# Cross attention: an output product with a new head sums the older head first and asks for the newer head's low part only at its last product

## The reference

```python
x = _rmsnorm(hidden_states, ln_weight)
h_q = (x @ w_q.T).reshape(b, lq, H, DH)                # H = 32, DH = 128, lq = lk = 128, b = 8
h_k = (key_value_states @ w_k.T).reshape(b, lk, H, DH)
h_v = (key_value_states @ w_v.T).reshape(b, lk, H, DH)
score = jnp.einsum('bqhd,bkhd->bhqk', h_q, h_k) + position_bias[None]
score = jax.nn.softmax(jnp.where(m, score, -jnp.inf), axis=-1)
attn = jnp.einsum('bhqk,bkhd->bqhd', score, h_v).reshape(b, lq, H * DH)
out = attn @ w_out.T
return hidden_states + out
```

## Time and profile before

| | |
|---|---|
| median of 3 runs | 1169.56 us (1166.43 to 1171.3) |
| profiled execution | 1164.94 us, of which span 1163.1 us |
| PE busy, PEld busy | 1113.6 us, 986.4 us |
| DVE, ACT, POOL busy | 536.7, 545.2, 223.6 us |
| mean granted PE clock | 0.987 of full |

### The profile page before, as it was taken

One profiled execution on the slowest core, in us unless ns is written; L12 is line 12 of the kernel. 1 busy time (PEld: TensorE's weight loads), 2 busy tenths in 40 slices (PEclk: granted clock), 3 DMA queues, 4 the chain that ended last, 5 costly groups with the idle time before them and its releaser, 6 DMA issues.

```text
span 1163.1 us, 20141 instructions
## 1 busy us (share of the span) xinstructions
PE 1113.6 (96%) x6904; PEld 986.4 (85%) x6904; DVE 536.7 (46%) x2002; ACT 545.2 (47%) x1342; POOL 223.6 (19%) x231
## 2 busy tenths in 40 slices
PE   4899999899999999999999999999999999999897
PEld 4899998798888888888888888888888888888785
DVE  3467777545344343434342434343343434343584
ACT  4687877434444444434443434434443434344412
POOL 5444544231010101010110101010101010111052
PEclk9899998899999999999999999999999999999999
DMA  3400100032020110101020202020211101000001
GB/s 138 158 10 11 47 2 2 28 137 78 1 77 25 52 58 18 59 18 59 18 72 5 77 0 77 0 77 1 75 35 41 59 18 59 18 23 1 1 2 72
DMA packets 16600, 49.63 MB, mean 43 GB/s; under 512 B 2480, under 2 KB 4912, under 8 KB 16048
## 3 DMA queue, kind: packets, MB, share of 16 engines
q1 hardware_dynamic: 16272, 44.93, 11.4%
q0 software_dynamic: 288, 4.19, 0.9%
HBM read 47.02 MB, written 2.10 MB: 42 GB/s over the span
## 4 chain that ended last, share of the span: by engine, by line
PE 88%; DVE 4%; ACT 3%; issue 3%; POOL 1%; DMA 1%; SPq 0%; ACTq 0%; POOLq 0%; DVEq 0%
PE bank L595 63%; PE bank L1238 5%; PE bank L1221 5%; PE bank L490 4%; PE bank L533 3%; PE bank L1260 3%; PE bank L1228 2%; PE bank L521 1%; DVE at_lo L1011 1%; ACT at_hi L861 1%; DMA stage<-in_wq 1%; PE bank L1298 1%; DVE sm L419 1%; POOL rot L290 0%; ACT pr L345 0%
## 5 line engine op out<-in xcount | busy, mean ns | idle before, releaser
L745 POOL TENSOR_TENSOR bm<-mask,bias 128x512 f32<-128x512 f32 x64 | 97.7, 1527 | 747.1 <-DVE nmx L999 483.9
L847 ACT ACTIVATE pr<-sm,nmx 128x128 f32<-128x128 f32 x256 | 99.8, 391 | 180.4 <-DVE nmx L999 180.2
L1011 DVE TENSOR_TENSOR at_lo<-bank,at_hi 128x512 fp32r<-128x512 f32 x64 | 44.2, 691 | 257.0 <-ACT at_hi L861 257.0
L1017 DVE TENSOR_TENSOR acc<-acc,bank 128x512 f32<-128x512 f32 x128 | 87.8, 687 | 138.9 <-PE bank L595 138.9
L840 ACT COPY v<-bank 128x256 f32<-128x256 f32 x128 | 47.8, 373 | 128.3 <-PE bank L595 77.0
L595 PE MATMUL bank<-wv_hi,cT_hi 128*128 128x256 f32 x512 | 92.5, 303 | 2.9 <-DVE wv_lo L985 2.9
L595 PE MATMUL bank<-wo_hi,at_hi 128*128 128x512 f32 x256 | 82.6, 404 | 11.1 <-DVE at_lo L1011 5.9
L595 PE MATMUL bank<-wv_lo,cT_hi 128*128 128x256 f32 x512 | 82.3, 283 | 0.0
L595 PE MATMUL bank<-wv_hi,cT_lo 128*128 128x256 f32 x512 | 82.2, 283 | 0.0
L834 ACT COPY kT<-bank 128x512 f32<-128x512 f32 x64 | 37.6, 588 | 90.7 <-PE bank L595 90.7
L419 DVE CUSTOM_DVE_ANT_0 sm<-bank,causal 128x128 f32<-128x128 f32 x256 | 58.8, 285 | 45.3 <-issue 41.8
(11 more groups left out here) (181 smaller groups left out, 2298.2 us busy)
## 6 DMA issues: line engine op xcount, KB each, us to landing
qk_raw<-in_wqk SPq DMA_DIRECT2D x32, 512.0 KB, 4.6
v_raw<-in_wv SPq DMA_DIRECT2D x16, 512.0 KB, 4.4
o_raw<-in_wo SPq DMA_DIRECT2D x16, 512.0 KB, 3.4
xT_raw<-in_xT SPq DMA_DIRECT2D x8, 256.0 KB, 2.8
acc<-in_x POOLq DMA_DIRECT2D x1, 2048.0 KB, 8.2
stage<-in_cT POOLq DMA_DIRECT2D x1, 2048.0 KB, 12.8
bias<-in_bias SPq DMA_DIRECT2D x16, 128.0 KB, 3.1
out<-acc SPq DMA_DIRECT2D x8, 256.0 KB, 2.0
```

What stands on the lines that cost most here:

```text
L745: nc.gpsimd.tensor_tensor(bm[:, s % 2], mask[:, HALF * (s // HG):HALF * (s // HG + 1), :], bias[:, s % HG:s % HG + 1, :].broadcast_to([P, ...
L847: e = nc.scalar.activation(pr[:, s % 2, k], sm[:, s % 2, k], ACT.Exp, bias=nmx[:, s % 2, k:k + 1], accum_out=sums[:, s % 2, k:k + 1])
L1011: nc.vector.tensor_tensor(at[1][:, s // HG, s % HG], PO[:], f32(at[0][:, s // HG, s % HG]), ALU.subtract).then_inc(s_al, 1)
L1017: nc.vector.tensor_tensor(acc[:, b], acc[:, b], PX[b % 2][:], ALU.add).then_inc(s_acc, 1)
```

## The change

`output` no longer calls `product`. It issues the same six matmuls, head by head: the three parts of head i = 0, then the three parts of head i = 1. Where it is the first output with a new head (`fresh`), the wait for `s_al` ahead of all six is gone; in its place the fourth matmul waits for `s_ah` and the sixth, which is the only one that reads the new head's low part, for `s_al`. All 128 outputs get the new order, 32 of them the new waits.

```diff
-            def output(b, half):
+            def output(b, half, fresh=None):
+
                 tok = slice((b - half * HALF) * T, (b - half * HALF + 1) * T)
-                product(nc, PX[b % 2][:], [[(at[p][:, half, i, tok], wo[q][:, i, :]) for i in range(HG)]
-                                           for p, q in PARTS]).then_inc(s_out, 1)
+                for i in range(HG):
+                    for p, q in PARTS:
+                        if fresh is not None and i == HG - 1 and (p, q) == PARTS[0]:
+                            pe.wait_ge(s_ah, fresh)
+                        if fresh is not None and i == HG - 1 and p == 1:
+                            pe.wait_ge(s_al, fresh)
+                        ins = nc.tensor.matmul(PX[b % 2][:], at[p][:, half, i, tok], wo[q][:, i, :],
+                                               start=i == 0 and (p, q) == PARTS[0],
+                                               stop=i == HG - 1 and (p, q) == PARTS[-1])
+                ins.then_inc(s_out, 1)
...
                     def out(j):
-                        if j == 0 and s in (0, 2):
-                            pe.wait_ge(s_al, n)
                         if j == 0 and s == 2:
                             pe.wait_ge(s_wo, g + 1)
-                        output((HALF + 2 * s + j) % B, 0 if s >= 2 else 1)
+                        output((HALF + 2 * s + j) % B, 0 if s >= 2 else 1, n if j == 0 and s in (0, 2) else None)
...
                     transpose_x2(0)
                     transpose_x2(1)
-                    pe.wait_ge(s_al, n)
                     for j in range(HALF):
                         pe.wait_ge(s_acc, 2 * n - 5 + j)
-                        output(HALF + j, 1)
+                        output(HALF + j, 1, n if j == 0 else None)
```

## The result

| | before | changed |
|---|---|---|
| median | 1169.58 us (4 runs, 1166.43 to 1171.3) | 1152.07 us (4 runs, 1148.18 to 1152.59) |
| ratio to before | | 0.9846, 95% interval 0.9816 to 0.9876 |
| profiled execution | 1164.94 us, span 1163.1 | 1152.29 us, span 1150.5 |
| first to last scores of the attention | 854.51 us | 835.61 us |

The change makes the kernel 17.5 us faster by the medians, 1.5%. The forecast was 1150.5 us and 19.0 us less.

What follows compares the result with a forecast made beforehand. PE, busy 96% of the span, was taken as the bound, so only its pauses could shrink. 15 x 0.66 + 15 x 0.61 + 0.26 = 19.3 us, or 18.6 by places, taken as 19.0, gave 1150.5 us; range 1145 to 1157.

Steps and rivals of the forecast that it cites:

- The price of a wait: Pause before the output product: 0.66 us in steps s = 0, 0.61 us in s = 2, against the s = 1 step.
- Who is late: Output products wait for DVE's at_lo, both in the 15 named waits and in the 15 unnamed ones of s = 2.
- The wait for the high part: At the output's fourth matmul, due at 519.80; high part complete at 518.79, 1.0 us before, so no cost.
- the satisfied waits in mid-stream: Waits already met inside the output's matmul stream: taken as free, at most 0.08 us for each of the two.
- the new order: Operands alternating between high and low parts over 768 matmuls: no cost, 3.8 us on either side.
- The cover of the low part: At the output's sixth matmul: low part released 0.37 us before the weight load is due, so the wait costs nothing.
- The sum: Total saved on PE's waits before outputs: 19.3 us by step lengths, 18.6 us by places, taken as 19.0 us.
- The end, counted at nothing: The 32nd wait, at the attention's end: nothing saved, since PE waits 0.73 us for xnT_lo a few us later.
- Weight loads uncovered by satisfied waits: Rival: each of 31 outputs gives back 2 x 0.08 us, 5.0 us in all, 1155.5 us; chance 0.08.
- A repeated load dropped: Rival: the second load of each head's high part falls away, 4.4 us more gained, 1146 us; chance 0.04.
- Half of the waits something else: Rival: unnamed waits of s = 2 are not for at_lo, so only 9.9 us go, 1159.7 us; chance 0.04.
- A slower order: Rival: part changes between neighbouring matmuls cost 0.08 us each, 61 us over 768, 1212 us; chance 0.04.

Runs made afterwards that it cites:

- order_only: Changed kernel keeping the new matmul order, but with the wait for the low part back ahead of all six; 1168.52 us, ratio 1.0003 to before.
- before_late_one: Kernel before the change, with one added DVE operation ahead of each low part; 1186.71 us, ratio 1.0127 to before.
- waits_only: Changed kernel with the old matmul order, waiting for the high part at the second matmul and the low part at the sixth; 1151.89 us, ratio 0.9864.
- low_at_fourth: Changed kernel with the low part awaited at the fourth matmul instead of the sixth, no wait for the high part; 1151.43 us, ratio 0.9878.
- after_late_one: Changed kernel with one added DVE operation ahead of each low part; 1149.47 us, ratio 0.9809 to before.
- after_again: Changed kernel run once more without any edit; 1151.81 us, ratio 0.9854 to before.
- before_again: Kernel before the change, run once more without any edit; 854.60 us from the first to the last scores.
- low_at_second: Changed kernel with the low part awaited at the second matmul instead of the sixth, no wait for the high part; 1160.02 us, ratio 0.9931.
- transposes_early: Changed kernel with the looped groups' transposes directly behind the scores, and ACT's copy of them ahead of its copy of k; 1151.40 us, ratio 0.9853.

## Why the prediction was right

**What bounds the kernel.** Right: the same matmuls and loads, and all of the gain in pauses of PE. The two busy totals, 1113.3 and 1113.6 us, don't show it; they agree by chance, as said above.

**The price of a wait, 0.66 and 0.61 us by step lengths.** Right. The looped steps s = 0 and s = 2 went to 13.38 or 13.39 us (but for the first, with its own wait), and `order_only` brings them back to 14.04 and 14.03 us. The wait view has only 0.39 us of it, because matmuls overlap in the trace: the last v block of the earlier trace rows is drawn until 518.63 + 0.64 = 519.27, 0.16 us beyond the 519.11 at which the output would have started. 0.39 + 0.16, and 0.08 for the first load, are 0.63 us.

**Who is late.** Right, for both kinds of step; `before_late_one` and the names in `order_only` show it.

**The wait for the high part, the satisfied waits in mid-stream and the new order cost nothing.** Right: the six matmuls come 0.23 us apart, `waits_only` and `low_at_fourth` have the same 835.6 us between the scores, and `order_only` is the kernel before.

**The cover of the low part.** Right that it suffices, too small by over a third: 0.37 us worked out, 0.59 us measured. The prediction did not need its size, only that there was some. Two terms were off. The release was taken at 0.15 us behind the low part, from a wait at the head of an output; on the matmul itself it takes 0.06 us. And the load was counted as late once it misses its usual start, while it may start some 0.13 us late before the next matmul is held (0.23 + 0.23 us from load to next matmul in the stream, 0.33 us when held). With both, 0.37 + 0.09 + 0.13 = 0.59 us. The weight load of `after_late_one` above shows the second term: 0.13 us late, and nothing held.

**The sum.** Between the scores 854.51 - 835.61 = 18.9 us, inside the 18.6 to 19.3 us of the two ways to add it up. The medians differ by 17.5 us, with an interval of 14.5 to 21.5 us by the ratio. In the other comparisons without a loss (`waits_only`, `low_at_fourth`, `after_again`) the medians differ by 17.1 to 17.5 us, so the totals fall 1 to 2 us short of the stretch each time. What is missing lies in the stages around it, which the change touches only at the end of the attention; whether it is chance, these runs don't tell. The profiled executions differ by 12.6 us only, which taken alone would have looked like a third of the gain lost. It wasn't: ahead of the first scores the changed kernel's execution took 245.1 us and that of before 240.2 us, and this is the spread that `before_again` (244.8) and the others show.

**The end, counted at nothing.** The 32nd wait did cost something, about 0.2 us, and the reason for counting it at nothing was wrong. In the trace of before, on PE and PEld:

```profile
1105.59 1.11 PE L1254 MATMUL bank<-ident,qk_raw 128*128 128x128 f32 x8 [1.65 <-DVE qk_raw L1031]
1106.65 0.30 PEld L595 LDWEIGHTS bank<-wo_hi,at_hi 128*128 128x128 f32 x2 [0.18 <-DVE at_lo L1011]
```

And in `after_late_one`, which has the new waits and ran this part at the full clock too:

```profile
1090.35 1.11 PE L1264 MATMUL bank<-ident,qk_raw 128*128 128x128 f32 x8 [2.25 <-DVE qk_raw L1032]
1091.22 0.48 PE L1252 MATMUL bank<-wo_hi,at_hi 128*128 128x512 f32 x1
```

From the transposes to the output 1.06 us pass in the first (both start at 1106.65) and 0.87 us in the second. The prediction had what is saved here wait at `xnT_lo`. But that wait ends at the same distance from the transposes that stand behind these outputs on PE, 4.52 us before (1112.15 to 1116.67) and 4.53 us in the changed kernel (1099.51 to 1104.04), so as far as the traces show it comes earlier with them and takes nothing back.

In the total this can't be seen: the stage behind the last scores took 69.7 us in place of 68.4, but `before_again` has 70.0 us. The longer time goes with the clock. Behind PE's pauses at the end of the attention a stretch of the changed kernel's trace runs at half rate, about 11 us behind the last scores, and so does one in `before_again`, about 12 us behind them, while the trace of before, with the same pauses, shows no such stretch until its last 5 us. All of the difference lies ahead of PE's wait for `xnT_lo`; from there to the end both the kernel before and the changed one take 46.4 or 46.5 us. Four microseconds each, first of the changed kernel, then of `before_again`:

```profile
1091.00:1095.00 4.00, 3.34 (x12) 3.04 (x13) 3.91 (x12) 1.17 (x2) 3.24 (x4) 0.57 0.00 0
```

```profile
1111.00:1115.00 4.00, 4.00 (x13) 3.05 (x12) 3.86 (x11) 1.07 (x2) 2.96 (x4) 0.58 0.00 0
```

The granted clock is 0.57 and 0.58 on average, so most of each stretch ran at 1.2 GHz and the rest at 2.4. In it the second, third and fourth matmul of the output come 0.42 and 0.43 us apart in the changed kernel:

```profile
1093.86 0.63 PE L1251 MATMUL bank<-wo_lo,at_hi 128*128 128x512 f32 x1
1094.28 0.63 PE L1251 MATMUL bank<-wo_hi,at_lo 128*128 128x512 f32 x1
1094.71 0.48 PE L1251 MATMUL bank<-wo_hi,at_hi 128*128 128x512 f32 x1
```

The Trainium skill (TensorE: Matmul & The Clock Gate, Wait — 56ns, not 53.3ns?) gives 426.7 ns between matmuls of 512 columns at the low clock; the trace agrees with it.

**The rivals.** Weight loads uncovered by satisfied waits: no step of 0.08 us anywhere in the six. A repeated load dropped: 6904 loads as before. Half of the waits something else: no, as `order_only` and `before_late_one` show. A slower order: no, by the steps of `order_only` without a wait, 13.39 us.

## What to carry to other kernels

A wait belongs at the first instruction that reads what it waits for, not at the head of the group; here, with PE at 96% busy, 31 such waits of 0.6 us were 1.6% of the time. Ask first which product of the group needs the late operand: here the order of the six could have stayed as it was. Price a wait from start to start against a sister step that lacks it: 0.4 us of shown idle time was 0.6 us of step. And compare the stretch that the change touches, since a stage that it doesn't touch moved by 5 us from run to run. A busy total that stays the same proves nothing either: here 7.8 us less in the attention and about as much more around it cancelled.

## What the runs showed of the hardware

- A wait that rides on a matmul in mid-stream let the load start 0.06 us behind the end of the DVE operation that it waits for; a wait at the head of the output, ahead of a matmul that has a second wait of its own, let PE start 0.15 us (s = 0) or 0.10 us (s = 2) behind it. Behind a held load the next matmul comes 0.33 us later (`low_at_second`), in the stream 0.46 us later, and a load that was 0.13 us late held nothing (`after_late_one`).
- From the scores to the transposes 0.89 us pass, from the scores to split products 0.81 us, though scores and transposes are both plain float32 (`transposes_early` and the changed kernel). What the 0.08 us are is open.
- The clock was granted differently from one execution to the next of one kernel: 0.94 and 0.92 on average in the stage ahead of the attention, which took 240.2 and 244.8 us, and a stretch of 4 us at 0.58 at the attention's end in one of the two. Over the twelve executions traced, the stage ahead of the first scores took 240.2 to 246.8 us.
